# Last stage of a decoder on one core: the second layer norm's arithmetic on ACT instead of DVE, its clip one step later

## The reference, cut to what matters

```python
def layer_norm(x):
    mean = jnp.mean(x, axis=-1, keepdims=True)
    var = jnp.var(x, axis=-1, keepdims=True)
    return (x - mean) / jnp.sqrt(var + EPS)          # EPS = 1e-6

def absmax_quant(x):
    gamma = jnp.max(jnp.abs(x), axis=-1, keepdims=True)
    x_hat = jnp.clip(x * Q_B / gamma, -Q_B + EPS, Q_B - EPS)   # Q_B = 128
    return x_hat * gamma / Q_B

def ternarize_weights(w):
    gamma = jnp.mean(jnp.abs(w))
    return jnp.sign(jnp.round(w / (gamma + EPS))) * gamma

def bitlinear(x, w):                  # forward value: absmax_quant(layer_norm(x)) @ ternarize(w).T
    ...
h = bitlinear(x, w_fc)                # 256 -> 1024
h = jax.nn.gelu(h, approximate=False)
y = bitlinear(h, w_proj)              # 1024 -> 256
x = _layernorm(x + y)                 # the decoder's own norm, eps 1e-5
```

## Time and profile before

| quantity | value |
|---|---|
| time, median of 3 runs | 4915.02 us (4914.43 to 4915.18) |
| the profiled execution's own time | 4917.29 us |
| its span | 4915.3 us |
| PE busy | 4447.4 us (90% of the span) |
| DVE busy | 3261.4 us (66%) |
| ACT busy | 2048.8 us (42%) |
| POOL busy | 1522.7 us (31%) |
| mean granted PE clock | 0.975 of full speed |

### The profile page before, as it was taken

The page is one execution under the profiler, slowest core; times in us unless marked ns, Lnnn a source line. Parts: engine busy times, 40 slices in busy tenths (PEclk is TensorE's granted clock), DMA queues, the critical chain, the costliest instruction groups (busy, mean ns, idle before and its releaser), DMA issues.

```text
span 4915.3 us, 87683 instructions
## 1 busy us (share of the span) xinstructions
PE 4447.4 (90%) x32598; PEld 3090.8 (63%) x32645; DVE 3261.4 (66%) x6084; ACT 2048.8 (42%) x4390; POOL 1522.7 (31%) x3050
## 2 busy tenths in 40 slices
PE   8998998799989898887799999999978999999788
PEld 6776887455546676776466666666655666666555
DVE  5667227788877678877555555555546666666798
ACT  4554113355544333333355555555533434343222
POOL 1111004433312233433344444444422222222122
PEclk9999998899999999999899999999999999999899
DMA  1003001344410100000000000000010000000000
GB/s 44 2 25 91 1 1 24 95 88 88 88 43 25 73 7 7 7 9 6 31 1 1 1 1 1 1 1 1 1 42 18 9 7 9 7 9 4 6 14 17
DMA packets 117700, 111.69 MB, mean 23 GB/s; under 512 B 22368, under 2 KB 110112, under 8 KB 112800
## 3 DMA queue, kind: packets, MB, share of 16 engines
q1 hardware_dynamic: 117280, 106.09, 8.3%
HBM read 88.48 MB, written 16.78 MB: 21 GB/s over the span
## 4 chain that ended last, share of the span: by engine, by line
PE 58%; issue 15%; DVE 15%; POOL 7%; ACT 4%; DMA 1%; SPq 1%; POOLq 0%; DVEq 0%; ACTq 0%
PE banks L2421 14%; PE banks L1279 5%; PE banks L2671 4%; PE banks L769 4%; POOL factors L2883 3%; PE banks L1910 3%; PE banks L1262 3%; PE banks L1155 2%; PE banks L2487 2%; PE banks L798 2%; PE banks L2587 1%; PE banks L1816 1%; PE banks L523 1%; PE banks L2515 1%; POOL mean_squares L2879 1%
## 5 line engine op out<-in xcount | busy, mean ns | idle before, releaser
L282 POOL TENSOR_TENSOR var_eps<-mean_var,ln_eps 128x1 f32<-128x1 f32 x384 | 83.3, 217 | 1309.2 <-DVE mean_var L278 959.3
L1319 ACT ACTIVATE exps<-banks 128x512 f32<-128x512 f32 x512 | 284.9, 595 | 259.1 <-PE banks L1262 258.9
L1167 DVE TENSOR_REDUCE neg_max<-banks 128x4 f32<-128x1024 f32 x256 | 311.2, 1217 | 98.4 <-PE banks L1155 98.1
L2442 ACT ACTIVATE squares<-banks 128x512 f32<-128x512 f32 x256 | 152.8, 597 | 441.4 <-PE banks L2421 441.4
L2475 DVE TENSOR_TENSOR q_normed<-banks,factors 128x512 f32<-128x512 f32 x256 | 176.3, 689 | 229.6 <-POOL factors L2465 229.3
L2859 ACT ACTIVATE squares<-q_normed 128x512 f32<-128x512 f32 x160 | 100.8, 630 | 396.6 <-DVE q_normed L2849 396.6
L2465 POOL TENSOR_TENSOR factors<-mean_squares,minus_half 128x4 f32<-128x4 f32 x256 | 258.5, 1010 | 21.5 <-POOL mean_squares L2461 0.3
L1910 PEld LDWEIGHTS banks<-yT,w_swiglu 128*128 128x128 f32 x2048 | 238.0, 193 | 30.0 <-issue 29.8
L1910 PE MATMUL banks<-yT,w_swiglu 128*128 128x128 f32 x2048 | 247.2, 277 | 8.4 <-DVE hidden L1934 8.4
L2421 PE MATMUL banks<-wq,x_turned 128*128 128x512 f32 x512 | 249.0, 609 | 3.0 <-ACT x_turned L2401 1.9
L284 POOL TENSOR_TENSOR rstd<-var_eps,minus_half 128x1 f32<-128x1 f32 x384 | 242.0, 630 | 30.1
(11 more groups left out here) (381 smaller groups left out, 11050.2 us busy)
## 6 DMA issues: line engine op xcount, KB each, us to landing
contextT<-in_ctxT SPq DMA_DIRECT2D x96, 128.0 KB, 2.5
parts_context<-parts SPq DMA_DIRECT2D x96, 64.0 KB, 2.2
parts_x<-parts SPq DMA_DIRECT2D x96, 64.0 KB, 2.0
stack<-parts_context SPq DMA_DIRECT2D x32, 192.0 KB
stack<-parts_x SPq DMA_DIRECT2D x32, 192.0 KB
x_all<-in_x SPq DMA_DIRECT2D x1, 4096.0 KB, 14.2
context<-in_ctx SPq DMA_DIRECT2D x64, 64.0 KB, 2.2
context<-in_ctx SPq DMA_DIRECT2D x32, 128.0 KB, 2.3
```

Source lines behind the costliest of these rows:

```text
L1167: v.tensor_reduce(self.mx[s][:, :, 2 * i:2 * i + 2].rearrange("p h g -> p g h"), self.bM[i % 2].rearrange("p g (h c) -> p g h c", h=DH), A ...
L1319: self.nc.scalar.activation(self.e[n % 8][:], self.bE[self.slot(t, n) % 2].rearrange("p (l c) -> p l c", l=DH), ACT.Exp, scale=self.TOK ** ...
```

## The change

The first instruction of the chain for the 1024 elements (`hidden_n`, `(x - mean) * rstd`) leaves DVE. ACT does the same arithmetic in place on the gelu buffer, as `Identity(rstd * g + shift)`, with `shift = -mean * rstd`, a new 128x1 POOL instruction. ACT's new phase `norm_act` has lag 2, between `down_act` and `p1_act`. The remaining six instructions of the chain stay on DVE and move from lag 2 to lag 3; everything behind them (the transposes, the second matmul, the tail) moves one step too, so the largest lag goes from 4 to 5. There are three gelu buffers instead of two, and the buffer `hidden_n` is gone. A gelu buffer is free for rewriting after the fifth of the six instructions.

```diff
-    def clip(self, wait, steps, t, xn, x, mv, rstd, q1, out, before_out):
+    def clip(self, link, xn, q1, out, before_out):
         v = self.nc.vector
-        link = Links(wait, steps, t)
-        link(v.tensor_scalar(xn, x, mv[:, 0:1], rstd[:, 0:1], ALU.subtract, ALU.mult))
         link(v.tensor_reduce(self.amax[:], xn, AX.X, ALU.max, apply_absolute_value=True))
...
     def p1_act(self, act, t, s):
         for c in (0, 1):
             act.wait_ge(self.made.sem, self.made.at(t, c + 1))
-            if c == 0 and begun(t - 2):
-                act.wait_ge(self.clip2.sem, self.clip2.all(t - 2))
-            self.nc.scalar.activation(self.g[s][:, c * 512:(c + 1) * 512], self.bG[c], ACT.Gelu, scale=self.gam[:, 0:1]).then_inc(self.gated.sem, 1)
+            if c == 0 and begun(t - self.GELUS):
+                act.wait_ge(self.clip2.sem, self.clip2.at(t - self.GELUS, 5))
+            self.nc.scalar.activation(self.gelu(t)[:, c * 512:(c + 1) * 512], self.bG[c], ACT.Gelu, scale=self.gam[:, 0:1]).then_inc(self.gated.sem, 1)
...
         pool.tensor_tensor(self.rs2[s][:], self.ve2[s][:], self.p.minus_half[:, 0:1], ALU.pow).then_inc(self.h_rs.sem, 1)
+        pool.wait_ge(self.h_rs.sem, self.h_rs.all(t))
+        pool.tensor_scalar(self.shift2[s][:], self.mv2[s][:, 0:1], self.rs2[s][:, 0:1], -1.0, ALU.mult, ALU.mult).then_inc(self.h_shift.sem, 1)
+
+    def gelu(self, t):
+        return self.g[t.index % self.GELUS]
+
+    def norm_act(self, act, t, s):
+        act.wait_ge(self.h_shift.sem, self.h_shift.all(t))
+        g = self.gelu(t)[:]
+        self.nc.scalar.activation(g, g, ACT.Identity, bias=self.shift2[s][:, 0:1], scale=self.rs2[s][:, 0:1]).then_inc(self.h_normed.sem, 1)
...
-        dve.wait_ge(self.h_rs.sem, self.h_rs.all(t))
-        self.clip(dve.wait_ge, self.clip2, t, self.hn[:], self.g[s][:], self.mv2[s], self.rs2[s], self.hq[:], self.h[s][:], free)
+        dve.wait_ge(self.h_normed.sem, self.h_normed.all(t))
+        self.clip(Links(dve.wait_ge, self.clip2, t), self.gelu(t)[:], self.hq[:], self.h[s][:], free)
...
-            "pe": [(3, self.down_pe), (1, self.p1_pe), (3, self.down_project), (0, self.p0_pe)],
-            "act": [(3, self.down_act), (1, self.p1_act), (0, self.p0_act)],
-            "dve": [(4, self.p4_dve), (0, self.in_stats), (2, self.p2_dve), (0, self.p0_dve), (1, self.p1_dve), (4, self.tail_scale)],
-            "pool": [(4, self.tail_pool), (0, self.in_pool), (1, self.p1_pool)],
+            "pe": [(4, self.down_pe), (1, self.p1_pe), (4, self.down_project), (0, self.p0_pe)],
+            "act": [(4, self.down_act), (2, self.norm_act), (1, self.p1_act), (0, self.p0_act)],
+            "dve": [(5, self.p4_dve), (0, self.in_stats), (3, self.p2_dve), (0, self.p0_dve), (1, self.p1_dve), (5, self.tail_scale)],
+            "pool": [(5, self.tail_pool), (0, self.in_pool), (1, self.p1_pool)],
```

More of the change, by code:

```diff
@@ L1578 @@
     EPS, Q = 1e-6, 128.0
+    GELUS = 3
     def __init__(self, plan, weights, source):
@@ L1595, in __init__ @@
         self.xc = [wk(f"x_clipped{s}", [P, D]) for s in (0, 1)]
-        self.g = [wk(f"gelu{s}", [P, H]) for s in (0, 1)]
+        self.g = [wk(f"gelu{n}", [P, H]) for n in range(self.GELUS)]
         self.st2 = [wk(f"hidden_stats{s}", [P, 12]) for s in (0, 1)]
@@ L1600, in __init__ @@
         self.rs2 = [wk(f"hidden_rstd{s}", [P, 1]) for s in (0, 1)]
-        self.hn = wk("hidden_n", [P, H]); self.hq = wk("hidden_clipped", [P, H])
-        self.clip1, self.clip2 = st("quantised", 7), st("quantised_hidden", 7)
+        self.hq = wk("hidden_clipped", [P, H])
+        self.shift2 = [wk(f"hidden_shift{s}", [P, 1]) for s in (0, 1)]
+        self.clip1, self.clip2 = st("quantised", 7), st("quantised_hidden", 6)
+        self.h_shift, self.h_normed = st("h_shift_ready"), st("h_normed")
         self.h_mv, self.h_ve, self.h_rs = st("h_mv_ready", 1), st("h_ve_ready"), st("h_rstd_ready")
@@ L1662, in p0_dve @@
         dve.wait_ge(self.n_rstd_ready.sem, self.n_rstd_ready.all(t))
-        self.clip(dve.wait_ge, self.clip1, t, self.xn[:], self.p.x_all[:, t.index, :], self.n_mv[s], self.n_rstd[s], self.q1[:], self.xc[s][:], free)
+        link = Links(dve.wait_ge, self.clip1, t)
+        link(self.nc.vector.tensor_scalar(self.xn[:], self.p.x_all[:, t.index, :], self.n_mv[s][:, 0:1], self.n_rstd[s][:, 0:1], ALU.subtract, ALU.mult))
+        self.clip(link, self.xn[:], self.q1[:], self.xc[s][:], free)
     def p0_pe(self, pe, t, s):
@@ L1699, in p1_dve @@
             dve.wait_ge(self.gated.sem, self.gated.at(t, c + 1))
-            v.bn_stats(self.st2[s][:, 6 * c:6 * c + 6], self.g[s][:, c * 512:(c + 1) * 512]).then_inc(self.h_sum.sem, 1)
+            v.bn_stats(self.st2[s][:, 6 * c:6 * c + 6], self.gelu(t)[:, c * 512:(c + 1) * 512]).then_inc(self.h_sum.sem, 1)
         dve.wait_ge(self.h_sum.sem, self.h_sum.all(t))
```

## The result

| | before | changed |
|---|---|---|
| median, first comparison (5 runs each) | 4914.54 us (4912.21 to 4915.18) | 4890.08 us (4888.24 to 4897.24) |
| changed over before | | 0.9953 (95%: 0.994 to 0.9967) |
| the profiled execution's own time | 4917.29 us | 4897.24 us |
| its span | 4915.3 us | 4895.5 us |
| mean granted PE clock | 0.975 | 0.974 |

The change makes the kernel 24.5 us faster by these medians, 0.50%; the interval of the ratio stands for 16 to 29 us.

What follows compares the result with a forecast made beforehand. DVE was taken to bound the last stage, PE second, 1.6 us behind. Terms -24.8 + 3.9 (drain) + 2.1 (clock) = -18.8 us from the median 4915.02 gave 4896.2 us, range 4893.0 to 4901.5.

Steps and rivals of the forecast that it cites:

- the period: DVE's time per tile in the last stage: 9.81 us less 0.81 for `hidden_n`, so 9.00 us, above PE's 8.21.
- the halt of PE: In step 3 PE, without its first round, idles 5.2 us until `x_clipped` of tile 3.
- three rounds at the end: After the last `x_clipped`, PE runs three rounds instead of two, each 4.84 us, following each other.
- The 29 periods: Steps 3 to 31: 29 x 0.81 = 23.5 us saved, with one residual and one `tail_scale` together 24.8 us.
- the drain: PE's work behind the last `x_clipped`: one more round costs 3.6 to 4.2 us, taken as 3.9.
- the clock term: After PE's halt in step 3 the clock halves for 6 us; DVE then waits once, losing 2.1 us.
- `in_stats` of step 3 at the same 4610.2: Start of the stretch where DVE runs without a wait: claimed unmoved by the change.
- a different start of step 3: Sign named beforehand: if `in_stats` of step 3 did not start at 4610.2, the prediction would be proved wrong.
- The one without a fall of the clock: Rival: no clock loss after PE's halt and the drain at its short end, 4893.8 us; chance 0.22.
- That DVE gives half the gain back: Rival: ACT's 128x1024 access stretches DVE by 0.4 us a tile, losing 11.6 us, 4907.8 us; chance 0.11.
- The clock that stays low: Rival: PE at half clock for four tiles, in steps 4 to 7, 4923.7 us; chance 0.05.
- a second table load: Rival: switching between `Gelu` and `Identity` makes ACT pay two table loads per tile; given no chance.

Runs made afterwards that it cites:

- the repetition: The changed kernel run once more with no edit, profiled again: median 4894.44 us (5 runs), ratio 0.9961; steady stretch 285.0 us.
- the third profile: Profile of the changed kernel's third set, again with no edit: median 4896.2 us, ratio 0.9954; steady stretch 283.4 us.

## Why the prediction was right, and where it was wrong

**Right, by the rows of after:** DVE as the bound, the period (9.00 forecast, 8.96 measured), ACT's instruction (1.25 and 1.24 us, at 2.9 after zero), PE's wait (0.8 and 0.76), the halt of PE (5.2 and 5.18), three rounds at the end (4.84 and 4.83), no wait for ACT in the steady state. That the clip must move a step for this to be a gain is shown by the kernel with the old lags. The mechanism is the one that was forecast.

**The terms.** For the steady stretch of the profiled execution the forecast's sum was -24.8 + 3.9 + 2.1 = -18.8 us; measured, -21.6. The 29 periods gave 24.8, and another 1.0 by the reduction's 34 ns; the drain cost 3.6; the clock 0.75. The sum -24.8 - 1.0 + 3.6 + 0.75 = -21.5 agrees. In the repetition, with 2.27 for the clock, it is -19.9, measured -20.1; in the third profile -21.6 again. So the clock term of 2.1 was mis-sized by 1.4 us, the drain by 0.3, and the missing term was the reduction's, 1.0. I had taken the length of the half clock (6 us) from one single case and as certain, and had let all of it fall on PE's work.

**The step that failed** is the last one: from the sum to a time and its range. The mis-sized terms alone would have stayed inside the range: with 21.6 us in place of 18.8 the same step gives 4893.4. "`in_stats` of step 3 at the same 4610.2" was the assumption that everything ahead of the change stays as it is in one profile. It started at 4612.0, 4607.6 and 4611.2 in three executions of the changed kernel, and at 4610.2 and 4604.1 in two of the kernel before; by the prediction's own sign ("a different start of step 3") it was wrong there. The low end of the range, 4893.0, was made of the change's own unknowns only and left nothing for this. Three sets of five runs of the same changed kernel had medians of 4890.08, 4894.44 and 4896.20; all 15 runs together have 4893.7, and the 67 runs of before 4915.1 (4907.6 to 4921.4). The difference of these two, 21.4 us, is that of the steady stretch. The 24.5 of the first set are 21.5 of mechanism and about 3 of scatter; the one is shown by the profiles, the other by the repetitions. That the third set's median is just the forecast's is luck, as is the first set's 2.9 us outside.

The scatter goes with the granted clock. Of the 15 executions of the changed kernel the five with a mean clock of 0.976 took 4888.2 to 4892.9 us, the ten with 0.973 to 0.975 took 4892.6 to 4897.6; four of the first set's five have 0.976, and one of the other ten. None of those five was profiled, so in which sections they are faster stays open; the transition can be one place.

**The rivals.** The one without a fall of the clock gave 4893.8, the nearest number, by the wrong way: the clock did fall, and cost less. That DVE gives half the gain back is refuted: the period fell by 0.85 us, a little more than the 0.81 taken away; `hidden_clipped` took 753 ns before and 754 after (medians of 32), the multiplication behind it 753 both times. The clock that stays low did not appear: full again after 3.4 or 6.8 us in all three profiles. Nor did a second table load: ACT's trace has one in this stage, at 4581.77 us.

"ScalarE: Activation LUTs" of the Trainium skill, "Rules for kernel authors", puts such arithmetic on VectorE. Here the instruction costs 1.24 us on ACT and 0.78 on DVE, as that rule has it, and yet moving it gained 0.85 us a tile, because ACT was idle. The estimate of 1.22 us for the instruction, worked out in the prediction from the same page's "What ACT_TABLE_LOAD costs", agrees with 1.24.

## What to carry to other kernels

Where one engine's list sets the period, an instruction can go to an idle engine that is slower at it, if its result is asked for one step later; on the same step the gain turns into a wait of the same size (0.75 of 0.81 us here). Price a longer pipeline by its drain and by the halt at its start, each by itself; the kernel with the longer pipeline alone paid 5.1 us for the two. And give the range the scatter of the whole program, not only the unknowns of the change: the median of five runs here moved by 6 us with nothing edited.

## What was not expected of the hardware

- The same instructions behind the same gaps (1.0 and 0.77 us) bring PE's granted clock to half in one execution and leave it at full in the next; this moved the start of step 3 by 4.3 us. The Trainium skill, "TensorE: Matmul & The Clock Gate", Part 1, says that the chip's watch over PE runs freely and does not start anew with a kernel, so that the moment of a change varies from run to run; these traces agree in that the moment varied (next item). It says this of a kernel's start; here it is the middle of a program, and even whether the clock falls varies.
- After the same halt of 5.18 us the clock was at half for 3.4, 3.4 and 6.8 us in three executions of one program. It fell 4.8, 4.7 and 4.5 us after PE had stopped, where the halt in the earlier trace rows showed 2.8.
- A DVE reduction over 128x1024 took 1186 ns on an input that had long been ready and 1220 on one that was written just before, by DVE or by ACT. That is not the whole rule: `residual` took 479 ns right behind `tail_scale` and 438 without it, though it doesn't read what `tail_scale` writes.
- An ACT `Identity` with both pointers over 128x1024 took 1.24 us. DVE's reduction over another buffer of that size ran beside it (they start at 4709.69 and 4710.14 in the rows of after) and took its 1186 ns.
